# A tuned transformer stack in one kernel: order of VectorE's and ScalarE's work at the start of the late cross-attention heads

## The reference

```
x = x + xattn(layernorm(x), ctx)            # ctx: 4096 x 512
q = (inputs_q @ Wq).reshape(.., 16, 128) / sqrt(128)
k = (inputs_kv @ Wk);  v = (inputs_kv @ Wv) # 16 heads of 128
attn = softmax(q k^T);  out = (attn @ v) @ Wo
```

## Time and profile before

| | us |
|---|---|
| median of three runs | 1713.86 (1710.75 to 1713.94) |
| the profiled execution | 1713.94 |
| its span in the trace | 1712.1 |
| TensorE busy | 1666.9 (97%) |
| VectorE busy | 1088.3 (64%) |
| ScalarE busy | 695.2 (41%) |
| GpSimd busy | 99.0 (6%) |

### The profile page before, as it was taken

The page is one execution under the profiler, slowest core; times in us unless marked ns, Lnnn a source line. Parts: engine busy times, 40 slices in busy tenths (PEclk is TensorE's granted clock), DMA queues, the critical chain, the costliest instruction groups (busy, mean ns, idle before and its releaser), DMA issues.

```text
span 1712.1 us, 23442 instructions
## 1 busy us (share of the span) xinstructions
PE 1666.9 (97%) x9232; PEld 1306.4 (76%) x9232; DVE 1088.3 (64%) x1746; ACT 695.2 (41%) x938; POOL 99.0 (6%) x183
## 2 busy tenths in 40 slices
PE   8998999999999999999999999998899999999998
PEld 7887888888788888888888888877658555544444
DVE  4445777777777777777777789995645805433333
ACT  3334444544444444445444455553312313222221
POOL 0000000000000000000000011111000000000000
PEclk9999999999999999999999999999899999999999
DMA  6755454445454555545445443234111437488880
GB/s 221 206 173 149 129 136 129 125 129 138 137 139 123 136 130 136 142 130 136 120 132 137 123 135 103 90 122 161 75 50 62 181 123 333 104 333 330 321 327 29
DMA packets 114765, 262.54 MB, mean 153 GB/s; under 512 B 6688, under 2 KB 76512, under 8 KB 108512
## 3 DMA queue, kind: packets, MB, share of 16 engines
q1 hardware_dynamic: 96224, 193.93, 36.7%
q0 software_dynamic: 18432, 67.12, 13.1%
HBM read 193.35 MB, written 67.67 MB: 152 GB/s over the span
## 4 chain that ended last, share of the span: by engine, by line
PE 73%; issue 16%; DVE 5%; DMA 2%; ACT 2%; POOL 2%; SPq 0%; DVEq 0%; POOLq 0%; ACTq 0%
PE bank L41 18%; PE bank L390 16%; PE bank L362 12%; PE bank L403 7%; PE bank L1885 5%; PE bank L1554 3%; PE bank L1906 2%; PE bank L1905 2%; PE bank L1914 2%; PE bank L135 1%; DMA v_dram<-v_out 1%; PE bank L428 1%; DVE e_lo L719 1%; POOL v_back L890 1%; DMA v_out<-in_wv 1%
## 5 line engine op out<-in xcount | busy, mean ns | idle before, releaser
L719 DVE TENSOR_TENSOR e_lo<-S,e_hi 128x1024 fp32r<-128x1024 f32 x128 | 156.5, 1223 | 91.8 <-ACT e_hi L548 91.2
L362 PE MATMUL bank<-cT_hi,wk_hi 128*128 128x512 f32 x512 | 205.3, 401 | 0.0
L390 PE MATMUL bank<-wv_hi,cT_hi 128*128 128x512 f32 x512 | 200.4, 391 | 3.5 <-DVE wv_lo L656 3.5
L362 PE MATMUL bank<-cT_hi,wk_lo 128*128 128x512 f32 x512 | 200.5, 392 | 0.0
L539 ACT ACTIVATE S<-S 128x1024 f32<-128x1024 f32 x128 | 135.7, 1060 | 158.9 <-DVE S L699 158.3
L390 PE MATMUL bank<-wv_hi,cT_lo 128*128 128x512 f32 x512 | 199.9, 390 | 0.0
L390 PE MATMUL bank<-wv_lo,cT_hi 128*128 128x512 f32 x512 | 199.7, 390 | 0.0
L362 PE MATMUL bank<-cT_lo,wk_hi 128*128 128x512 f32 x512 | 199.2, 389 | 0.0
L548 ACT CAST e_hi<-S 128x1024 fp32r<-128x1024 f32 x128 | 134.7, 1052 | 143.2 <-PE bank L403 136.3
L712 DVE TENSOR_TENSOR esum<-esum,S 128x512 f32<-128x512 f32 x210 | 144.9, 690 | 71.2 <-ACT S L539 67.6
L403 PE MATMUL bank<-e_hi,v_back 128*128 128x256 f32 x880 | 168.3, 289 | 4.2 <-DVE e_lo L719 3.5
(11 more groups left out here) (271 smaller groups left out, 2845.0 us busy)
## 6 DMA issues: line engine op xcount, KB each, us to landing
w<-in_w_moe SPq DMA_DIRECT2D x32, 2304.0 KB, 8.6
v_dram<-v_out SPq DMA_DIRECT2D x112, 512.0 KB, 4.6
v_back<-v_dram POOLq DMA_DIRECT2D x110, 512.0 KB, 5.0
v_dram<-v_back SPq DMA_DIRECT2D x16, 512.0 KB, 3.9
ctx_nat<-in_ctx SPq DMA_DIRECT2D x8, 1024.0 KB, 4.9
ctx_raw<-in_ctxT SPq DMA_DIRECT2D x7, 1024.0 KB, 8.0
v_late<-v_dram POOLq DMA_DIRECT2D x14, 512.0 KB, 3.5
l_w_qkv<-in_l_wqkv SPq DMA_DIRECT2D x6, 1024.0 KB, 5.5
```

The lines of the kernel that those rows point to most:

```text
L362: t = e.matmul(banks[b][:], l, r, start=(c == 0 and m == 0), stop=(c == DT - 1 and m == 2))
L390: t = e.matmul(banks[b][:], l, r, start=(c == 0 and m == 0), stop=(c == DT - 1 and m == 2))
L719: e.tensor_tensor(lo[:], Sj, hi[:].bitcast(F32), ALU.subtract).then_inc(e_split, 1)
```

## The change

The order of calls in the hand-written loops of ScalarE and VectorE is changed, for h = 12 to 14 and, on VectorE, for h = 15. No instruction is added or removed; TensorE, GpSimd and SyncE keep their lists.

```diff
 # scalar_cross, for h in range(LATE, XH - 1), after move_o(h - 1)
                 round_k(h + 1, 0)
-                raise_scores(h, 0)
-                round_e(h, 0)
                 round_k(h + 1, 1)
-                raise_scores(h, 1)
-                round_e(h, 1)
-                store_scores(h + 1, 0)
+                for j in (0, 1):
+                    raise_scores(h, j)
+                    round_e(h, j)
                 for j in range(1, NCH):
                     if j + 1 < NCH:
                         raise_scores(h, j + 1)
-                    if j > 1:
-                        store_scores(h + 1, j - 1)
+                    store_scores(h + 1, j - 1)
...
 # vector_cross, for h in range(LATE, XH - 1)
                 split_q(h + 1)
+                fold_sum(h - 1)
                 keep_max(h, NCH - 1)
-                fold_sum(h - 1)
+                split_k(h + 1, 0)
                 shift(h, 0)
-                split_k(h + 1, 0)
+                split_k(h + 1, 1)
                 shift(h, 1)
+                sum_e(h, 0)
                 split_e(h, 0)
                 invert_sum(h - 1)
-                sum_e(h, 0)
-                split_k(h + 1, 1)
+                add_head(h - 1)
+                sum_e(h, 1)
                 split_e(h, 1)
-                sum_e(h, 1)
                 shift(h, 2)
-                add_head(h - 1)
...
 # vector_cross, h = XH - 1
+            fold_sum(h - 1)
             keep_max(h, NCH - 1)
-            fold_sum(h - 1)
             own.wait(e)
             shift(h, 0)
             shift(h, 1)
-            invert_sum(h - 1)
             for j in range(NCH):
                 split_e(h, j)
-                if j == NCH // 2:
+                if j == 0:
+                    invert_sum(h - 1)
                     add_head(h - 1)
```

## The result

The changed kernel takes 1722.92 us (median of four runs, 1721.35 to 1724.41) against 1712.86 us of the kernel before measured beside it (1710.75 to 1713.94): a ratio of 1.006, 95% interval 1.0043 to 1.0078. It is slower by more than the 0.2% that can be told.

A forecast was written before the change was run, and what follows sets the result against it. TensorE, busy 97% of the 1712.1 us span, was taken as the bound. Heads +9.5, last head -0.9 and -2.0 made 6.6, with the clock's +5.0 11.6: from 1713.94 to 1725.5 us, range 1718.5 to 1729.

The forecast's parts named there:

- the clock: Heads 12 to 14: one fall to half clock after each new TensorE idle, +5.0 us; bounds 0 and 3.3 per head.
- the losses of the three heads together: Starts of heads 12, 13 and 14: 3.15 us lost per head, +9.5 us for three, without the clock.
- The late copy: Head starts: chunk 1 scores wait for ScalarE's copy of chunk 0 scores, now behind exponential 2; new idle 2.75 us.
- The walk: Start of h = 13, standing for three: instruction-by-instruction timing of TensorE, ScalarE and VectorE in their new order; 3.15 us lost.
- a smaller one of 0.7: Late heads: a TensorE idle of 0.7 us in front of each head's first weighing.
- The rival in which the clock holds: Late heads: no fall of the clock, or one; 1720.5 us, up to 1722.2 with one fall; chance 0.22.
- The last head: Head 15: gains of -0.9 us at the last chunk's scores and -2.0 us from the earlier sum onward.
- -0.9: Head 15, scores of the last chunk: the 0.87 us wait for VectorE's K split goes.
- -2.0: Head 15: first weighing 2.27 us earlier, a wait of 1.2 replacing 0.97; bounds 0 and -3.2.
- the second term: Head 15, the -2.0: fold_sum ahead of keep_max lets output matmuls start 2.1 us earlier; first weighing 2.27 earlier.
- The rival on the other side: Head starts: chunk 0 scores leave PSUM by 1065.2, so only gains stay, 1709.5 us; chance 0.06.

The follow-up runs named there:

- e1: Changed kernel with ScalarE's copy of the next head's chunk 0 scores put back ahead of the exponential of chunk 2: median 1713.09 us, ratio 0.9991 to before.
- e2: Kernel before with only ScalarE's half of the diff, VectorE as before: median 1724.45 us, ratio 1.0061 to before.
- e3: Kernel before with only VectorE's half of the diff, ScalarE as before: median 1721.02 us, ratio 1.004 to before.
- e4: Changed kernel with 11 filler matmuls on TensorE in front of each late head's second scores: median 1719.86 us, ratio 1.0034 to before.
- e7: Kernel before with fold_sum ahead of keep_max in the last head, add_head later there and in heads 12 to 14: median 1710.36 us, ratio 0.9979.
- e6: Kernel before with only VectorE's edits of the last head, h = 15: median 1710.32 us, ratio 0.998 to before.
- e5: Changed kernel with add_head moved back behind shift 2: median 1716.39 us, ratio 1.0015 to the kernel before.

## Why the prediction was right, and where its terms were off

The forecast was 1725.5 us for the profiled execution's kind of run, 11.6 more than before; it came to 10.6 there (1724.57), and the median is 2.6 us under the forecast. The total is closer than its terms, since their errors have opposite signs: the clock was put 2.1 us too high, and the losses of the three heads together 0.7 too low. How many falls the profiled execution would have was partly luck.

*The late copy.* Right, and e1 shows it. The walk gave an idle of 2.75 (2.69 measured), a smaller one of 0.7 (0.84), and the scores of chunk 1 at 3.67 late (3.90 in head 12: 4.09 less the 0.19 at the start). Per head 3.15 was forecast and 3.39 measured. Of the 0.24, 0.2 are add_head's wait for the reciprocal, which the walk had as a step of 0.08.

*The clock.* That a fall can follow the new idles was right, its size was not: +5.0 was forecast, 2.9 measured. Two falls came where I had three, and one costs 1.42 (4.81 - 3.39, head 13) to 1.47 (4.86 - 3.39, head 14) and not 1.65. The timeline of head 13 shows why: a matmul of 256 columns is issued every 0.12 us at full clock (1057.45 to 1057.57 in e1), not twice as fast as at half, 0.21 to 0.22 (1073.66 to 1073.88 to 1074.09 here). Half the clock is less than twice the time, and an estimate from these steps, 3.3 times (1 - 0.12 / 0.215) = 1.46 us, meets what was measured:

```profile
1073.66 0.41 PE L41 MATMUL bank<-q_hi,k_lo 128*128 128x256 f32 x1
1073.88 0.41 PE L41 MATMUL bank<-q_lo,k_hi 128*128 128x256 f32 x1
1074.09 0.63 PE L403 MATMUL bank<-e_hi,v_late 128*128 128x256 f32 x2
```

Nor is a fall sure. Of the idles of 2.4 to 2.7 us in the profiled executions here, two of three were followed by one in the changed kernel, one of three in e2 (2.37, 2.36, 2.36), one of three in e3 (2.69 each). The median, 1722.92, lies between what the prediction gave for one fall (1722.2) and for two (1723.8). The rival in which the clock holds was thus half right, and its time (1720.5, up to 1722.2 with one fall) is as near to the fastest run (1721.35) as the forecast is to the slowest. The Trainium skill, "TensorE: Matmul & The Clock Gate", section "Why this matters for your kernels", warns only of longer gaps. The runs disagree with it as a rule for safety: four of these nine shorter gaps were followed by a fall, and e4, which does nothing but fill them, won 2.8 us in the late part.

*The last head.* -0.9 and -2.0 were forecast, 2.9 together; 13.25 to 10.44, or 2.8, came back. The sum was right, but the reason given for the second term was not. Two small things were missed: the first weighing also waits for the reciprocal, which now stands behind E split 0 (1.58 <- small), and GpSimd started its reduction 0.3 later behind its DMAs. The prediction calls the fall of the clock in this place before covered by filler. It was not: the filler took 5.17 us where it takes 4.18 in e2 at full clock, and the first weighing stands behind it. e2 happened to run this place without the fall, with the same wait of 2.54 in front: its lag shrinks there from 9.79 (last weighing of head 14) to 8.14 (first of head 15), 1.65 us. So of the 2.27 by which the prediction had the first weighing start earlier, 1.65 is that fall, and what the edits of the last head win depends on whether it comes.

*The rival on the other side*, that the copy is not what TensorE waits for, would have needed the chain of VectorE's and ScalarE's steps up to the copy to be 2.75 us too long. The chain was wrong by 0.2, and e1 shows the copy as the cause.

## What to carry to other kernels

On an in-order engine ask of each moved instruction not what it needs but what the one in front of it needs: the copy had its data some 9 us before it ran (scores issued by 1061.5, copy at 1070.67). Where two engines share a single buffer, look whether its emptying can stand ahead of anything that waits on a third; here that place was worth 10.5 us. Where an engine is the bound of a stretch, moving its work about inside the stretch can just move the wait (e7). Cutting the longest wait at the stretch's end from 2.54 to 0.46 us paid (e6), by estimate 0.3 us for the waits themselves and 1.65 for the fall that did not follow.

## What the runs showed of the hardware

- An idle of TensorE of 2.4 to 2.7 us in the midst of work was followed by 3.3 us at the granted clock of 0.50 in some executions and heads and not in others, with the same instructions around it; none of the idles of 0.8 to 1.75 us in the late part of these profiles was. Behind the late part one was: in e2 the clock fell at 1198.6, behind idles of 1.64 and 0.32 us, and the same idles in the kernel before (1188.98 and 1190.40) were not followed by one. So no length of idle in these profiles is shown to be safe.
- Filling such an idle with 22 instructions into an unused bank kept the clock at 1.00 in all three heads of the profile (e4), and the late part was 2.80 us shorter than with two falls.
- At half clock back-to-back matmuls of 256 columns came every 0.21 us against 0.12 us: a fall of 3.3 us cost 1.42 to 1.47, not 1.65.
- On VectorE, add_head behind the reciprocal that it needs started 0.27 us after the reciprocal's start (1064.40 to 1064.67), where the sum of E, which does not need it, starts 0.08 after it (1063.55 to 1063.63 in e5).
